# A transformer block on 32 batches: maxima turned on DVE and spread by ACT, attention output packed by transfers and scaled there

## What is computed

```python
ada = silu(c) @ W_ada + b_ada
shift_msa, scale_msa, gate_msa, shift_mlp, scale_mlp, gate_mlp = split(ada, 6)
h = layernorm(x) * (1 + scale_msa) + shift_msa
q, k, v = heads(h @ W_qkv + b_qkv)
attn = softmax(q @ k.T * 18 ** -0.5)
x = x + gate_msa * ((attn @ v) @ W_proj + b_proj)
h = layernorm(x) * (1 + scale_mlp) + shift_mlp
x = x + gate_mlp * (gelu(h @ W_fc1 + b_fc1) @ W_fc2 + b_fc2)
```

## Time and profile before

| | |
|---|---|
| median of 3 runs | 1312.5 us (1309.87 to 1312.69) |
| profiled execution: time | 1315.15 us |
| profiled execution: span, first to last instruction | 1313.4 us |
| busy: PE, PEld, DVE, ACT, POOL | 1276.1, 1163.0, 876.3, 717.5, 476.6 us |
| instructions in the span | 29412 |
| DMA: moved, mean | 146.07 MB, 111 GB/s |
| granted clock of TensorE, mean | 0.996 of 2.4 GHz |

### The profile page before, as it was taken

One profiled execution on the slowest core, in us unless ns is written; L12 is line 12 of the kernel. 1 busy time (PEld: TensorE's weight loads), 2 busy tenths in 40 slices (PEclk: granted clock), 3 DMA queues, 4 the chain that ended last, 5 costly groups with the idle time before them and its releaser, 6 DMA issues.

```text
span 1313.4 us, 29412 instructions
## 1 busy us (share of the span) xinstructions
PE 1276.1 (97%) x11079; PEld 1163.0 (89%) x11079; DVE 876.3 (67%) x2085; ACT 717.5 (55%) x1165; POOL 476.6 (36%) x522
## 2 busy tenths in 40 slices
PE   6889999999999999999999999999999999999996
PEld 5668999999999999999999999999999999999886
DVE  4587766666677676667666677666666666766642
ACT  3266565556555555556555655555565655555541
POOL 2013334343333334333434333333433333433344
PEclk9999999999999999999999999999999999999998
DMA  8343333333243333334333333343333433333210
GB/s 255 121 133 109 117 121 114 112 107 118 91 133 114 115 105 106 112 111 130 111 109 108 115 96 127 115 120 106 101 121 100 132 111 112 98 110 93 84 39 19
DMA packets 83081, 146.07 MB, mean 111 GB/s; under 512 B 12471, under 2 KB 51417, under 8 KB 82942
## 3 DMA queue, kind: packets, MB, share of 16 engines
q1 hardware_dynamic: 82942, 144.18, 35.0%
HBM read 96.31 MB, written 47.30 MB: 109 GB/s over the span
## 4 chain that ended last, share of the span: by engine, by line
PE 93%; DVE 3%; ACT 1%; DMA 1%; issue 1%; SPq 1%; POOL 0%; POOLq 0%; ACTq 0%; DVEq 0%
PE x_bank L479 10%; PE a_bank L589 10%; PE score_bank L509 9%; PE st_bank L537 9%; PE turn_bank L548 9%; PE b_bank L589 8%; PE b_bank L603 6%; PE b_bank L605 6%; PE b_bank L604 6%; PE a_bank L570 5%; PE x_bank L492 5%; PE score_bank L522 2%; PE a_bank L457 2%; PE turn_bank L556 2%; PE a_bank L460 1%; PE x_bank L457 1%
## 5 line engine op out<-in xcount | busy, mean ns | idle before, releaser
L836 DVE TENSOR_REDUCE mx<-score_bank 128x2 f32<-128x512 f32 x512 | 337.7, 686 | 198.9 <-PE score_bank L509 196.7
L666 ACT ACTIVATE e<-st_bank 128x1024 f32<-128x1024 f32 x256 | 262.8, 1026 | 111.8 <-PE st_bank L537 107.8
L972 POOL TENSOR_TENSOR gl<-gl_raw,gh 128x512 fp32r<-128x512 f32 (+1 forms) x160 | 188.5, 1179 | 182.6 <-DVE gh L899 182.6
L603 PE MATMUL b_bank<-w,gh 128*128 128x288 f32 x576 | 176.5, 306 | 0.7 <-DVE tmp L905 0.6
L509 PE MATMUL score_bank<-kl,ql 108*128 108x256 f32 x1024 | 171.5, 289 | 2.1 <-ACT mxs L660 2.1
L537 PE MATMUL st_bank<-ql,kl 110*128 110x256 f32 x1024 | 170.1, 288 | 0.6 <-ACT e L666 0.5
L605 PE MATMUL b_bank<-w,gl 128*128 128x288 f32 x576 | 170.5, 296 | 0.0
L604 PE MATMUL b_bank<-w,gh 128*128 128x288 f32 x576 | 170.3, 296 | 0.0
L509 PEld LDWEIGHTS score_bank<-kl,ql 108*128 108x128 f32 x1024 | 141.1, 190 | 15.8 <-issue 15.8
L537 PEld LDWEIGHTS st_bank<-ql,kl 110*128 110x128 f32 x1024 | 140.3, 190 | 4.9 <-issue 1.1
L548 PE MATMUL turn_bank<-e,ve 128*32 128x256 f32 x2048 | 137.5, 386 | 0.0
(11 more groups left out here) (145 smaller groups left out, 2591.1 us busy)
## 6 DMA issues: line engine op xcount, KB each, us to landing
qk_rows<-qst SPq DMA_DIRECT2D x128, 256.0 KB, 2.5
ql<-qk_rows SPq DMA_DIRECT2D x384, 72.0 KB
kl<-qk_rows SPq DMA_DIRECT2D x384, 72.0 KB
gate<-gates SPq DMA_DIRECT2D x32, 432.0 KB, 4.8
xin<-in_x SPq DMA_DIRECT2D x32, 288.0 KB, 3.0
x<-in_x SPq DMA_DIRECT2D x32, 288.0 KB, 3.3
out<-x SPq DMA_DIRECT2D x32, 288.0 KB, 3.4
qk_rows<-qst SPq DMA_DIRECT2D x32, 128.0 KB, 4.9
```

What stands on the lines that cost most here:

```text
L603: nc.tensor.matmul(b_bank[:, 0:C], gh[:, cols], w2[:, 0, f, :], start=(f == 0), stop=False)
L666: nc.scalar.activation(e[:, j % 4, :, :, :].rearrange("p i u l -> p (i u l)"), st_bank[:, :, :, :].rearrange("p i u l -> p (i u l)"), ACT. ...
L836: nc.vector.tensor_reduce(mx[:, b % 2, :, col:col + 1], score_bank[i][:, :].rearrange("p (t l) -> p t l", t=NT), AX.X, ALU.max).then_inc(s ...
L972: nc.gpsimd.tensor_tensor(gl[:, cols], g[:, cols], gh[:, cols].bitcast(F32), ALU.subtract).then_inc(g_lo, 1)
```

## The change

The maxima no longer go through PE, a copy and a transfer. `mx` now has 32 columns for each half, head of the pair and tile of 128 rows; DVE transposes it in blocks of 32 x 32 (`mt`, one instruction per half), and ACT spreads the result into four rows of `ql`, one per pair of the half, with eight copies of 4 rows x 256 (`mb`). `kl` holds -1 in row 64 + j of pair j alone, and the rows of Q and K lie around these (0 to 53 and 68 to 121; the second head of a pair starts at 68). A thirteenth read of each half fills the four rows of `ql` with zeros from HBM, so that `s`, which now has the full depth too, sees no maximum. In code, `KM` is 122.

`e` is laid out so that `st` is two matmuls of 512 columns per pair in the place of four of 256. `pv` runs once per half, 32 matmul steps into both halves of `turn_bank`.

The output is not turned back. ACT copies a half of it, with the sums, to `on_sb`. SP stores it in HBM (`ow`, two transfers per half) and moves the sums within SBUF to 64 partitions x 32 (`sr`); DVE takes the reciprocals (`rcp`), and SP stores them (`sw`). ACT issues the reads: six that bring the output back, packed as 7 heads x 18 rows, the same again, and two heads in a remainder (`or`), and six that bring each head's reciprocals, repeated on its 18 rows (`rr`). DVE multiplies (`om`), ACT rounds (`oh`), POOL and DVE make the low parts (`ol`). `proj` takes `oh`, `ol` and `orem`, with 126, 126 and 119 rows, so `ot`, `on`, `onat` are gone and `xh3`, `xl3`, `xr3` belong to the MLP alone. `xl1` and `xl3` now lie on `v1` and `v3`. W_proj is loaded in rows that fit this. The splitting of the weights on DVE moves from batch 0 (`on`) to batch 1 (`max`).

All five lists are new; those of PE, ACT, DVE and SP stand in the diff, in this order. Of the diff, constants, semaphores, the loading of W_proj and the call's HBM tensors are left out, and so are the functions taken out, which stand among those above. `OT` is 126, `OREM` 119, `TH` 7, and `O_REM` lists the four pieces of the remainder.

```diff
 PE_ORDER = [
...
+    ("fc2", -3, 4), ("lt", -2, 1), ("pv", -1, 1), ("s", 0, 4), ("fc2", -3, 5), ("fc1", -2, 0), ("qk", 1, 0),
+    ("s", 0, 5), ("fc1", -2, 1), ("qk", 1, 1), ("st", 0, 0), ("s", 0, 6), ("fc1", -2, 2), ("fc1", -2, 3),
+    ("fc1", -2, 4), ("qk", 1, 2), ("s", 0, 7), ("fc2", -2, 0), ("fc2", -2, 1), ("st", 0, 1), ("v", 1, 0),
+    ("st", 0, 2), ("proj", -1, 0), ("st", 0, 3), ("v", 1, 1), ("proj", -1, 1), ("s", 1, 0), ("pv", 0, 0),
+    ("s", 1, 1), ("st", 0, 4), ("fc2", -2, 2), ("xt", 2, 0), ("st", 0, 5), ("s", 1, 2), ("fc2", -2, 3), ("st", 0, 6),
+    ("lt", -1, 0), ("xt", 2, 1), ("s", 1, 3), ("st", 0, 7),
 ]
...
 ACT_ORDER = [
...
+    ("st", -1, 6), ("lt", -2, 0), ("st", -1, 7), ("lt", -2, 1), ("xt", 1, 1), ("or", -1, 0), ("pv", -1, 1),
+    ("mb", 0, 0), ("fc1", -2, 0), ("qk", 1, 0), ("rr", -1, 0), ("or", -1, 1), ("or", -1, 2), ("fc1", -2, 1),
+    ("or", -1, 3), ("qk", 1, 1), ("or", -1, 4), ("or", -1, 5), ("rr", -1, 1), ("rr", -1, 2), ("fc1", -2, 2),
+    ("rr", -1, 3), ("rr", -1, 4), ("rr", -1, 5), ("fc1", -2, 3), ("fc1", -2, 4), ("st", 0, 0), ("qk", 1, 2),
+    ("oh", -1, 0), ("st", 0, 1), ("oh", -1, 1), ("v", 1, 0), ("st", 0, 2), ("st", 0, 3), ("mb", 0, 1), ("v", 1, 1),
+    ("pv", 0, 0), ("st", 0, 4), ("st", 0, 5), ("xt", 2, 0),
 ]
...
+    ("max", 0, 2), ("max", 0, 3), ("sum2", -3, 0), ("ln2_apply", -2, 0), ("ln2_apply", -2, 1), ("max", 0, 4),
+    ("max", 0, 5), ("xt", 1, 0), ("max", 0, 6), ("max", 0, 7), ("mt", 0, 0), ("lt", -2, 0), ("xt", 1, 1),
+    ("rcp", -1, 0), ("lt", -2, 1), ("max", 0, 8), ("max", 0, 9), ("sum2", -3, 1), ("rcp", -1, 1), ("qk", 1, 0),
+    ("max", 0, 10), ("fc1", -2, 0), ("max", 0, 11), ("fc1", -2, 1), ("qk", 1, 1), ("fc1", -2, 2), ("max", 0, 12),
+    ("max", 0, 13), ("max", 0, 14), ("om", -1, 0), ("ln1_stats", 2, 0), ("qk", 1, 2), ("om", -1, 1), ("fc1", -2, 3),
+    ("ol", -1, 1), ("ln1_apply", 2, 0), ("max", 0, 15), ("proj", -1, 0), ("mt", 0, 1), ("fc1", -2, 4),
+    ("ln1_apply", 2, 1), ("proj", -1, 1), ("max", 1, 0), ("max", 1, 1), ("ln2_stats", -1, 0),
...
+    ("qkw", 0, 3), ("qkr", 0, 0), ("qkr", 0, 1), ("qkr", 0, 2), ("qkr", 0, 3), ("qkr", 0, 4), ("qkr", 0, 5),
+    ("qkr", 0, 6), ("qkr", 0, 7), ("qkr", 0, 8), ("qkr", 0, 9), ("qkr", 0, 10), ("qkr", 0, 11), ("qkr", 0, 12),
+    ("qkw", 0, 4), ("qkr", 0, 13), ("qkr", 0, 14), ("qkr", 0, 15), ("qkr", 0, 16), ("qkr", 0, 17),
+    ("ln1_stats", 3, 0), ("qkr", 0, 18), ("qkr", 0, 19), ("ow", -1, 0), ("qkr", 0, 20), ("qkr", 0, 21),
+    ("qkr", 0, 22), ("sr", -1, 0), ("qkr", 0, 23), ("qkr", 0, 24), ("ow", -1, 1), ("qkr", 0, 25), ("sw", -1, 0),
+    ("sr", -1, 1), ("ow", -1, 2), ("ow", -1, 3), ("store", -3, 0), ("sw", -1, 1), ("qkw", 1, 0), ("qkw", 1, 1),
+    ("res", -1, 0), ("qkw", 1, 2),
 ]
...
+        mx = sb("mx", [P, HALVES, 2, NT, VB])
+        mxt = sb("mxt", [P, HALVES, 2, NT, VB])
         ve = sb("ve", [P, 2, NT, H, VB])
...
+        e = sb("e", [P, 4, NT, 2, L])
...
+                if m == 12:
+                    if use == 0:
+                        sp.sem_inc(qk_rows[slot], 16)
+                    else:
+                        sp.wait_ge(zeros_stored, 16)
+                        sp.dma_start(ql[MXR:MXR + HP, slot, :, :, :].rearrange("p i j l -> p (i j l)").bitcast(F32),
+                                     zero_dram).then_inc(qk_rows[slot], 16)
...
+            def ow(b, n):
+                half, q = n // 2, n % 2
+                sp.wait_ge(turn_drained, HALVES * b + half + 1)
+                if n == 0 and b >= 2:
+                    sp.wait_ge(o_rows[b % 2], 32 * (b // 2))
+                    sp.wait_ge(o_rem_rows[b % 2], 16 * len(O_REM) * (b // 2))
+                sp.dma_start(o_dram[b % 2, half, :, q], on_sb[:, q, :]).then_inc(o_stored[half], 16)
+            def sum_read(b, half):
+                wait(sp, rc_ready, HALVES * (b - 1) + half + 1)
+                sp.wait_ge(turn_drained, HALVES * b + half + 1)
+                sp.dma_start(sums[P // 2 * half:P // 2 * (half + 1), :],
+                             on_sb[D:P:VB, :, :].rearrange("c q l -> c (q l)").rearrange("c (x i) -> c x i", i=VB)
+                             ).then_inc(sums_loaded[half], 16)
+            def rc_write(b, half):
+                sp.wait_ge(rc_ready, HALVES * b + half + 1)
+                if half == 0 and b >= 2:
+                    sp.wait_ge(rc_rows[b % 2], 32 * (b // 2))
+                    sp.wait_ge(rc_rem_rows[b % 2], 16 * len(O_REM) * (b // 2))
+                sp.dma_start(r_dram[b % 2, half].rearrange("c q (x i) -> (c q x) i", i=VB),
+                             rc[P // 2 * half:P // 2 * (half + 1), :]).then_inc(rc_stored[half], 16)
...
+                if j % HP == 0:
+                    pe.wait_ge(mx_rows, HALVES * b + j // HP + 1)
                 if b == 0 and j == 0:
                     pe.wait_ge(gates_ready, 3)
                     pe.wait_ge(mod_ready, 2)
                 wait(pe, e_ready, PAIRS * b + j)
-                for i in range(2):
+                for u in range(NT):
+                    last = nc.tensor.matmul(st_bank[:, u, :, :], kl[0:KM, slot, j % HP, u * P:(u + 1) * P],
+                                            ql[0:KM, slot, :, j % HP, :], start=True, stop=True)
+                last.then_inc(st_full, 1)
+            def pv(b, half):
+                pe.wait_ge(e_ready, PAIRS * b + HP * (half + 1))
+                if half == 0:
+                    pe.wait_ge(x_drained, X_USES * (b + 1))
+                wait(pe, turn_drained, HALVES * b + half)
...
+                        for c in range(4):
+                            last = nc.tensor.matmul(turn_bank[VB * c:VB * (c + 1), q * L:(q + 1) * L],
+                                                    ve[:, b % 2, u, 8 * half + 2 * c + q, :],
+                                                    e[:, c, u, q, :],
+                                                    start=(u == 0), stop=(u == NT - 1))
...
+                pe.wait_ge(o_lo, b + 1)
+                pe.wait_ge(o_rem, b + 1)
+                wait(pe, a_drained, A_USES * b + USE_PROJ + t)
+                pr = products(oh, ol, orem, wp, OT, OREM)
...
+            def mb(b, half):
+                slot, _use = half_use(b, half)
+                act.wait_ge(mx_turned, HALVES * b + half + 1)
+                rows = ql[MXR:MXR + HP, slot, :, :, :].rearrange("p i j (t a x) -> p i j t a x", t=NT, x=VB)
+                for t in range(NT):
+                    for a in range(P // VB):
+                        src = mxt[VB * a:VB * a + HP, half, :, t, :].unsqueeze(2).broadcast_to([HP, 2, HP, VB])
+                        last = nc.scalar.copy(rows[:, :, :, t, a, :], src)
+                last.then_inc(mx_rows, 1)
...
+            def pv(b, half):
+                act.wait_ge(turn_full, HALVES * b + half + 1)
+                before = (b, 0) if half else (b - 1, 1)
+                if before[0] >= 0:
+                    act.wait_ge(o_stored[before[1]], 32 * (before[0] + 1))
+                    act.wait_ge(sums_loaded[before[1]], 16 * (before[0] + 1))
+                nc.scalar.copy(on_sb[:, :, :], turn_bank[:, :].rearrange("p (q l) -> p q l", l=L)).then_inc(turn_drained, 1)
+            def oh_copy(b, n):
+                act.wait_ge(o_scaled, 2 * b + n + 1)
                 if n == 0:
-                    nc.scalar.copy(xh3[:, :, :].rearrange("p c l -> p (c l)"), a_bank[:, :]).then_inc(o_hi, 1)
+                    wait(act, a_full, A_USES * (b - 1) + USE_PROJ + NT)
+                    nc.scalar.copy(oh[0:OT, :, :], ol_raw[0:OT, :, :]).then_inc(o_hi, 1)
                 else:
-                    nc.scalar.copy(xr3[0:KR, :], a_bank[0:KR, 0:L]).then_inc(o_hi, 1)
+                    nc.scalar.copy(orem[0:OREM, :], orem_raw[0:OREM, :]).then_inc(o_hi, 1)
+            def o_place(dst, dst_rem, n):
+                if n < 2:
+                    return dst[0:OT, n, :], TH * n, TH
+                r0, w0, nr = O_REM[n - 2]
+                return dst_rem[r0:r0 + nr, :], w0 // D, nr // D
+            def rc_read(b, n):
+                if n == 0:
+                    wait(act, o_scaled, 2 * b)
+                    act.wait_ge(rc_stored[0], 16 * (b + 1))
+                    if b == 0:
+                        act.wait_ge(consts, FIRST_SET)
+                if n == 1:
+                    act.wait_ge(rc_stored[1], 16 * (b + 1))
+                to, h0, nh = o_place(rcb, rcb_rem, n)
+                src = r_dram[b % 2].rearrange("f c q l -> (f c q) l")[h0:h0 + nh].unsqueeze(1).broadcast_to([nh, D, L])
+                act.dma_start(to, src).then_inc((rc_rows if n < 2 else rc_rem_rows)[b % 2], 16)
+            def o_read(b, n):
+                if n == 0:
+                    wait(act, a_full, A_USES * (b - 1) + USE_PROJ + NT)
+                    act.wait_ge(o_stored[0], 32 * (b + 1))
+                    if b == 0:
+                        act.wait_ge(consts, FIRST_SET)
+                if n == 1:
+                    act.wait_ge(o_stored[1], 32 * (b + 1))
```

(32 more changed lines are left out.)

276 lines of the change are left out of this document (128 added, 148 removed), and 21 rows, old and new, of tables (ACT_ORDER, DVE_ORDER, PE_ORDER, POOL_ORDER).

## The result

The changed kernel takes **1378.28 us** (median of 4 runs, 1375.49 to 1386.99) against 1312.11 for the kernel before (4 runs, 1309.87 to 1312.69): a ratio of 1.0519, 95% interval 1.0469 to 1.0569. It is slower by 5%, where the prediction had 4% faster. The profiled execution took 1375.49 us, with a span of 1373.7.

What follows compares the result with a forecast made beforehand. PE, busy for 97% of the span, was taken as the bound: 38.7 us per batch less 2.9 of work plus 1.1 of waits gives 36.9. Over 29 full periods that is -52 us: 1263, or 1260 on the median's scale (1245 to 1275).

Steps and rivals of the forecast that it cites:

- my own sum: Whole kernel: 29 full periods at 36.9 instead of 38.7 us, -52 us, with filling and emptying unchanged.
- PE's work: TensorE per batch: removed transposes, fewer probability-times-V calls and wider score matmuls take 2.9 us off 38.7, leaving 35.8.
- The wide matmuls: Transposed scores on PE: 16 matmuls of 512 columns for 32 of 256 save 0 to 0.2 us, 0.1 taken.
- The stalls: PE waiting between transposed score steps for the exp on ACT: 1.1 us per batch, possibly 0 to 1.6.
- my second rival: Transposed scores on PE: 512-column matmuls at 0.13 us save 1.7 us, period about 35.9, near 1230 us; chance 0.02.
- At 2.5, the last read ... is hidden, by 2 us: Output and reciprocal reads: last one lands at 19.5 us of the period, multiplied by DVE about 21.7, hidden in full periods.
- a rival alone: The rival on ACT's transfer waits: one hop takes 4.9 instead of 2.5 us, using up the 2 us; chance 0.18.
- Spreads at 0.30 and issues at 0.35: New ACT work per batch: 16 spread copies of maxima, 4.8 us, and 12 transfer issues, 4.2 us.
- ACT's sum: ScalarE's busy time per batch: 29.4 us (25 to 32), 80% of the 36.9 period, so it fits.
- I put the ends at 0: Filling and emptying of the pipeline: no net change, with 8 us either way.
- ACT slips: ACT's in-order transfer waits: late hops or dearer issues pass 0.4 to 1 us to PE; period 38.0, about 1292; chance 0.18.
- A few DMA engines saturate: New transfers cut by heads load the first DMA engine 35.5 us per batch; period 39.5, 1336 us, slower; chance 0.11.

Runs made afterwards that it cites:

- e2: Changed kernel with the gates' reload left out from batch 2 on (later batches use gates of batches 0 and 1): 1313.21 us.
- e5: Changed kernel with the gates' load split, its first third issued ahead of SP's run of stores and loads, the rest behind it: 1337.61 us.
- e10: Changed kernel with the gates' load split and moved, and each half's output stored as four transfers of 32 rows of 2 KB: 1323.09 us.
- e6: Changed kernel with seven of the eight spread copies of each half's maxima on ACT left out from batch 2 on: 1366.60 us.
- the wide stores: Changed kernel with each half's output stored as four transfers of 32 rows of 2 KB instead of two of 4 x 32 rows: 1366.26 us.
- e9: Kernel before the change with the gates' reload left out from batch 2 on: 1313.49 us, ratio 0.9993 to 1.0018.

## Why the prediction was wrong

Measured against my own sum, the span should have been 1313.4 - 52 = 1261 and was 1373.7: 112 us off. By parts: 24 full periods at 39.98 instead of 36.9, 74 us; the filling, 29; the rest, 10 (of the 29 full periods of my sum, one lies in this filling and four in the rest, so 1.8 and 7.2 us of these are gains that didn't come).

- **PE's work: nearly right.** Predicted 35.8 us and a floor of 36.9. Without the late reads the period is 37.4, of which PE is busy for 36.8. The wide matmuls save nothing, where I had 0.1. The stalls, sized at 1.1, are 0.6 us of idle time, ahead of the projection and not of an st. Those for the exp are there too, but counted as busy: in e2 two st of a batch take 0.60 to 0.73 instead of 0.47, and their weight load waited for the exp (48 times between 223.5 and 1150 us, twice a period). That is about half of the 1.0 us by which PE's busy time lies over my sum; the rest I have not located. The 131 ns of my second rival were not seen: two 512-column matmuls take 0.47, 235 ns each. For a 512-column matmul in a stream with its weight loads the Trainium skill ("TensorE: Matmul & The Clock Gate", section on the back-to-back issue gap) states 131 ns, and 216 ns for an isolated one; the first does not fit here, and the second is 8% short.
- **"At 2.5, the last read ... is hidden, by 2 us": the step that failed.** The read landed in 7.2 us. I took 2.5 from the kernel before, a median mostly of stores that stand apart from the gates' load, and put the new reads into the burst without counting what SP issues in those same 4.3 us. The slowest kind in the earlier trace rows, at 4.9, is the 128 KB store that follows x and the gates: the price of that place was in my rows, and I gave it to a rival alone. The Q/K stores, too, went from 2.5 to 5.1 us to landing. The margin of 2 us became a deficit: DVE waited for this read in 30 of 32 batches, PE behind it in 27. Of the 2.6 us by which a period exceeds 37.4, e2 gives back 2.4, e5, with the same bytes, 1.3.
- **The price of a late read: missing.** I let a slip pass on to PE at most one for one. In e10 a read 1.4 us later goes with 3.3 us, of which 1.4 are 3.4 us at 1.2 instead of 2.4 GHz, right behind PE's idle 2.5 us.
- **Spreads at 0.30 and issues at 0.35: mis-sized.** 0.40 and 0.67. ACT's sum becomes 22.1 - 2.9 + 1.2 + 6.4 + 8 = 35 of 40 us, not 29.4 of 36.9. e6 puts the price of 5.8 us of it at 0.4 per period.
- **"I put the ends at 0": the second step that failed.** The filling costs 27.5 us. My working compared only what the first batches have to compute. The traces show it otherwise: PE is idle for 14.6 and 5.5 us of the first two periods, and the chain of the first runs through the landing of the output's store (4.72 us), nine reads' issues on ACT and the landing of the last read (6.68), that of the second through the landing of a read (7.00). These belong to a new loop that stands in order on ACT, SP, DVE and PE, and in these periods there is little MLP work to lie beside it. That this loop sets their length is my reading; what of it decides is open. Moving the reads' issue, the projection or the scores back each made the filling longer, and leaving six reads out showed nothing beyond what the third period varies by. One further difference was not tried by itself: the kernel before has ("qk", 2, 0) and ("qk", 2, 1) in PE's list, the changed one ("qk", 1, 0) and ("qk", 1, 1), so that a batch's Q and K are made in the iteration that wants its first scores.
- **The rivals.** "ACT slips" named the right mechanism, a hop that takes longer, and stopped at 4.9 us and 38.4 per period, with the sign still wrong. "A few DMA engines saturate" had the sign and nearly the period (39.5), by a cause that is a smaller part: the cut of the stores is worth 12 us alone and 14.5 with a lighter burst, and the mean DMA share stayed near 45%. The packets bear out the cut: the wide stores have 3584 more on q1 at equal bytes (112435 instead of 108851), which is 256 x 16 - 128 x 4, as if there were one packet more per transfer and engine. By the section of "DMA: Bandwidth & Descriptors" that the prediction names in the Trainium skill, four pieces go to four engines; this count agrees.

## What to carry to other kernels

Before a transfer is put on the critical path, list everything that any queue issues within its flight time, and take its landing time from a row under such a load. A median over all transfers of a kind hides it: ask for those that are issued in the same place (here 4.9 us against 2.5). If its place can't move, move the bulk loads: splitting one 432 KB load and shifting 288 KB more gave back 65 of 66 us here (with wider stores), at equal bytes. A step taken off the bounding engine can be paid for in the filling if its replacement is a round trip in the lists of several in-order engines: count the filling's periods by the longest loop too, and not only by the work in them.

## What was not expected of the hardware

- The place of one 432 KB load that writes 128 partitions from the same three rows decides over 41 us in the changed kernel (e5); in the kernel before, leaving the load out altogether changes nothing (e9). The DMA engines' mean share is under 0.5 in both.
- In e10, 2.5 us of PE idle are followed by 3.4 us at 1.2 GHz, and the period's 307 matmuls take 1.4 us more; with 0.6 us idle the clock stays at 2.4 GHz.
- In the kernel before, Q/K stores behind the gates' load land in some 4.7 us and others in 2.5; without that load (e9) the 128 KB one takes 3.8 instead of 4.9.
- Copies of 4 rows x 256 on ACT take 403 ns, the same as one of 128 x 288 in this run (402).
- Issues on ACT's queue took 0.32 to 0.82 us each in the period shown, while SP issued too.
